# Dense experts by tiles of 512 text columns with two image tiles, and smaller edits around them, in a two-layer fusion kernel

## The reference

```python
# x: (16, 3, 96, 96), x_txt: (16, 512)
h = concat([patches(x) @ tok_W.T + tok_b, table[x_txt] + pe])     # (16, 548, 64)
h = h + attn0(layernorm(h))      # R = x + relu(q k.T) v ; layernorm(R + relu(R w1 + b1) w2 + b2)
h = h + moe0(layernorm(h))       # top 1 of 8, hidden 256, capacity ceil(1.25 T / 8)
# layer 1, attention
qkv = h1 @ W_qkv.T + b_qkv       # k, v normalised by head of 4, with gains and biases
kv  = einsum('bhnd,bhne->bhde', k, v) / HW
h   = h + gelu((q kv + h1) @ W_proj.T + b_proj) + h1             # h1 = layernorm(h)
# layer 1, experts
weights, top_idx = top_2(softmax(xt @ Wr + br))
xe = norm(xt) * ln_g[e] + ln_b[e]
y  = gelu(xe @ W1[e] + b1[e]) @ W2[e] + b2[e]                    # e = 0..7, hidden 256
out = h + sum of weights * y[top_idx]
```

## Time and profile before

| | us |
|---|---|
| median of 3 runs (lowest, highest) | 857.36 (856.84, 860.45) |
| profiled execution | 856.15 |
| its span | 854.3 |

### The profile page before, as it was taken

One profiled execution on the slowest core, in us unless ns is written; L12 is line 12 of the kernel. 1 busy time (PEld: TensorE's weight loads), 2 busy tenths in 40 slices (PEclk: granted clock), 3 DMA queues, 4 the chain that ended last, 5 costly groups with the idle time before them and its releaser, 6 DMA issues.

```text
span 854.3 us, 16008 instructions
## 1 busy us (share of the span) xinstructions
PE 727.0 (85%) x4863; PEld 542.2 (63%) x4863; DVE 586.5 (69%) x2216; ACT 490.5 (57%) x923; POOL 436.5 (51%) x457
## 2 busy tenths in 40 slices
PE   4599999999973399735599999999999999999994
PEld 3467777777752266524377776677767777777773
DVE  2658898998886255656777777877778777765421
ACT  1356656565622266403377777667866678775652
POOL 4743547783655400265647666576666754223321
PEclk9599999999975599955589999999999999999998
DMA  8900000000000122200112321122202222022220
GB/s 244 362 15 11 9 15 22 22 19 3 5 4 3 45 87 88 62 20 8 24 37 55 62 62 33 31 62 63 62 16 49 62 63 60 10 54 62 62 61 13
DMA packets 49534, 43.69 MB, mean 51 GB/s; under 512 B 19962, under 2 KB 45066, under 8 KB 49066
## 3 DMA queue, kind: packets, MB, share of 16 engines
q1 hardware_dynamic: 40666, 36.33, 16.6%
q0 software_dynamic: 7200, 4.17, 2.2%
q10 hardware_dynamic: 1584, 2.18, 0.8%
HBM read 31.65 MB, written 13.47 MB: 53 GB/s over the span
## 4 chain that ended last, share of the span: by engine, by line
PE 45%; DVE 14%; ACT 9%; issue 7%; DMA 0%; DVEq 0%; POOL 0%; POOLq 0%; ACTq 0%
PE psum L521 9%; PE psum L1012 8%; PE psum L1013 6%; ACT scratch L607 3%; PE psum L1199 3%; PE psum L496 2%; PE psum L990 2%; ACT L607 2%; ACT L553 2%; PE psum L983 2%; PE psum L447 2%; DVE stats L1354 2%; PE psum L1181 1%; DVE xt L680 1%; DVE mv L1357 1%
## 5 line engine op out<-in xcount | busy, mean ns | idle before, releaser
L607 ACT ACTIVATE scratch<-psum,fb 128x584 f32<-128x584 f32 x256 | 177.3, 744 | 97.8 <-PE psum L1013 95.7
L422 POOL TENSOR_TENSOR prob<-prob,scratch 128x292 f32<-128x292 f32 x112 | 81.2, 725 | 150.1 <-DVE scratch L852 145.4
L521 PE MATMUL psum<-scratch,w_fw 128*64 128x292 f32 (+1 forms) x1024 | 143.0, 401 | 0.1
L382 POOL DMA_INDIRECT uu<-expert_out,slot_i x80 | 82.9, 1036 | 86.6 <-issue 77.0
L1012 PE MATMUL psum<-kh,fw_hi 128*128 128x292 f32 x352 | 105.7, 323 | 10.8 <-ACT scratch L607 10.7
L943 POOL DMA_INDIRECT slots_buf<-xt,slot_i x80 | 81.8, 1022 | 57.6 <-DVE slot_i L1594 36.0
L521 PEld LDWEIGHTS psum<-scratch,w_fw 128*64 128x64 f32 x1024 | 89.4, 136 | 27.6 <-DVE scratch L852 5.2
L1013 PE MATMUL psum<-kh,fw_lo 128*128 128x292 f32 x352 | 93.0, 291 | 0.0
L929 POOL DMA_INDIRECT emb<-in_table,w_ids x64 | 63.0, 984 | 54.3 <-DVE stats L1354 33.2
L1012 PEld LDWEIGHTS psum<-kh,fw_hi 128*128 128x128 f32 x352 | 66.8, 190 | 27.3 <-ACT scratch L607 16.0
L1256 ACT ACTIVATE prob<-psum 128x292 f32<-128x292 f32 (+1 forms) x160 | 54.9, 396 | 30.5 <-PE psum L1066 30.5
(11 more groups left out here) (262 smaller groups left out, 1696.1 us busy)
## 6 DMA issues: line engine op xcount, KB each, us to landing
X<-share_buf SPq DMA_DIRECT2D x16, 584.0 KB, 5.9
X<-share_buf SPq DMA_DIRECT2D x16, 512.0 KB, 7.7
slots_buf<-zeros SPq DMA_DIRECT2D x8, 352.0 KB, 4.4
expert_out<-zeros SPq DMA_DIRECT2D x8, 352.0 KB, 4.2
X<-slots_buf SPq DMA_DIRECT2D x16, 128.0 KB, 2.0
expert_out<-X SPq DMA_DIRECT2D x16, 128.0 KB, 1.7
out<-H SPq DMA_DIRECT2D x16, 128.0 KB
X<-in_patches ACTq DMA_DIRECT2D x1, 1728.0 KB, 7.0
```

The costliest lines, as they stand in the source:

```text
L382: pool.indirect_dma_start(yg[b % 2][0:rows, s, :], None, expert_out, bass.IndirectOffsetOnAxis(slot_i[0:rows, b, (s + 1) % SLOTS:(s + 1) % ...
L422: pool.tensor_tensor(total[b % 2][:, 0:RIGHT], total[b % 2][:, 0:RIGHT], part[m % PARTS], ALU.add).then_inc(sem("summed"), 1)
L521: last = pe.matmul(bank(6 + n % 2)[h * D:(h + 1) * D, 0:z], w["fw2"][:, e * J + j, :], hid[(J * n + j) % (J * UNITS)][:, h, 0:z], start=(j ...
L607: act.activation(hid[(J * n + j) % (J * UNITS)], both(2 + 2 * j), ACT.Gelu, bias=fb1[:, e * J + j:e * J + j + 1]).then_inc(sem("gelu"), 1)
```

## The change

The dense experts run by tiles. A batch's 512 text columns are one tile, and the image tokens of batches 0 to 13 (2 x 252 columns) and of batches 14 and 15 (2 x 36 columns) are tiles 14 and 16 of 18. The columns in sum stay the same. An up product covers 512 columns into one bank, the halves go round over banks 2 to 5, and gelu reads 512 columns; down, weigh and the sums are 256 columns wide.

```diff
-                banks.take(pe, (2 + 2 * j, 3 + 2 * j), sem("gelu"), J * n + j + 1)
+                m = J * n + j
+                banks.take(pe, (2 + m % 4,), sem("gelu"), m + 1)
                 k = (e * J + j) * P
-                for h, z in enumerate(SIDES):
-                    last = two(pe, bank(2 + 2 * j + h)[:, 0:z], split["fw1"], xs5[b % XS5][:, h * ODD:h * ODD + z], slice(k, k + P))
-                last.then_inc(sem("up"), 1)
+                two(pe, bank(2 + m % 4)[:, 0:2 * width(t)], split["fw1"], tile_x(t), slice(k, k + P)).then_inc(sem("up"), 1)
```

```diff
+                for s in range(TXT):
+                    at0 = s % 2 * LEFT + s // 2 * P
+                    pe.matmul(bank(1)[:, s * 2 * E:(s + 1) * 2 * E], xs5[b % XS5][:, at0:at0 + P], wr_both[:], start=True, stop=True)
...
-                st(dve.tensor_tensor(lg[:], by_slot(1, E), bc(ratio[b % 2][:], E), ALU.mult))
+                st(dve.tensor_tensor(lg_pair[:], by_slot(1, 2 * E), bc(ratio[b % 2][:], 2 * E), ALU.mult))
+                st.sync()
+                st(dve.tensor_tensor(lg[:], lg_pair[:, :, 0:E], lg_pair[:, :, E:2 * E], ALU.add))
...
+                dve.tensor_tensor(xs5[b % XS5][other, cols], bank(1)[side, 0:LEFT], xs5[b % XS5][side, cols].bitcast(F32), ALU.subtract).then_inc(sem("xs5"), 1)
```

The gains of v move from a second product with a copy in front (p1_s) to two operations of own_heads on DVE. Fills are added, products of ones that nobody reads:

```diff
+        def fill(pe):
+
+            banks.left(pe, FILLED)
+            for _ in range(3):
+                pe.matmul(bank(FILLED).rearrange("p (k n) -> p k n", k=4), ones_b[:], bs(ones_b[:], 4), start=True, stop=True)
```

```diff
-        B_STEPS = [(e, c) for c in range(0, ET, 4) for e in range(E)]
+        B_STEPS = [(e, c, t) for c, t in ((0, 3), (3, 2), (5, 4), (9, 2)) for e in range(E)]
...
-        FIRST_UNITS = 2 * E
+        NEEDED_UNITS = (2 * E, 3 * E, NU)
...
+            def low_moe(_):
+                dve.wait_ge(sem("high_w"), 2)
+                dve.tensor_tensor(split["fw1"][1][:], fw1, split["fw1"][0][:].bitcast(F32), ALU.subtract).then_inc(sem("low_moe"), 1)
```

```diff
+            for k in range(KC):
+                if k % (KC // PATCH_LOADS) == 0:
+                    pe.wait_ge(sem(f"patches_in{k // (KC // PATCH_LOADS)}"), 16)
+                for h in range(2):
+                    last = pe.matmul(bank(h)[h * D:(h + 1) * D, 0:NB * N_IMG // 2], w["tok_w"][:, k, :], patches[:, k, h * NB * N_IMG // 2:(h + 1) * NB * N_IMG // 2],
...
+            act.activation(sd3[0][:, 0:1], eps_t[:, 0:1], ACT.Sqrt)
```

```diff
+        DVE_MOVED = {("add_input", 0): 3, ("add_input", 2): 0.5, ("finish", 17): 16, ("fold", 14): 2, ("fold", 15): -2, ("fold", 2): 0.75,
...
-        MOE, SQUEEZE_TWO, DOWN_LAG, GELU_LAG, WEIGH_LAG, SUM_LAG = 171.5, {}, 1.25, 0.5, 2.5, 0
+        MOE, DOWN_LAG, GELU_LAG, WEIGH_LAG, SUM_LAG, BACK_LAG, FINISH_LAG = 170, 1.5, 0.75, 2.5, -0.5, 12.75, 12
-        B_START, B_STEP, B_READY = -34.5, 2.7, -60
+        B_START, B_STEP, B_READY = -9, 2, -82
```

482 lines of the change are left out of this document (298 added, 184 removed), and 16 rows, old and new, of tables (ACT_MOVED, DVE_MOVED, PE_MOVED).

## The result

The changed kernel takes 847.75 us (median of four runs, 846.61 to 849.94) where the kernel before takes 857.87 beside it: a ratio of 0.9881, 95% interval 0.985 to 0.9911. That is 10 us faster. I had forecast 783 with a range from 750 to 815: right about the sign, wrong about the size by a factor of seven. The profiled execution of after took 848.33 us, 7.8 less than that of before.

A forecast was written before the change was run, and what follows sets the result against it. PE was taken to set the pace in phase 1 and the dense stage, a chain over four engines at half clock between. Terms -6 - 1 - 7 - 14 - 46 = -74 gave 782.2 us profiled, 783 median, range 750 to 815.

The forecast's parts named there:

- A, start: Start up to phase 1: patch products in two column groups and image tokens in halves, -6 us (-1 to -8).
- B, body: Body of phase 1: no operation changes, at most half of PE's missing 6 us returns, -1 us (0 to -3).
- C, end of the first part: End of phase 1 to first unit's turn: shorter waits, fills holding the clock up (4 us), -7 us (-2 to -11).
- D, first turn to first up: First unit's turn to first dense unit: gather waits less, clock gives 10 us, -14 us (-4, clock unchanged, to -20).
- E, dense stage: Dense stage: PE needs 21.1 us a batch, period 22.7 instead of 26.95, -46 us (-25 to -67).
- with the starts still there: Dense stage: a pair of units takes 4.4 us if slower starts remain, 3.84 without waits and starts.
- Rival 2: Dense stage: DVE operations stretched beside POOL become the bound, 3.3 us more a batch, 826 us; chance 0.20.
- Rival 3: Dense stage: latency of one batch's chain sets the period, above 28.4 us, kernel slower (872 at 29.5); chance 0.03.

The follow-up runs named there:

- e17: Kernel before with extra unused PE products in the dense stage, 5.1 us a batch: ratio 1.0939 to the kernel before, period 32.15 us.
- e7: Kernel before with ACT's roots4 moved early, beside the other Sqrt stages: ratio 1.002 to the kernel before, period 27.2 us.
- e1: Changed kernel with the first part's plan tables as before the change: 840.6 us, ratio 0.9793 to the kernel before.
- e2: Changed kernel without the 44 fills (PE products whose result nobody reads): 845.2 us, ratio 0.9854 to the kernel before.
- e13: Changed kernel with extra unused PE products in the dense stage, 5.1 us a batch: ratio 1.065 to the kernel before, period 29.06 us.
- e16: Kernel of e9 with the same extra PE products, 5.1 us a batch: ratio 1.0545 to the kernel before, period 29.25 us.
- e3: Changed kernel with ACT's roots4 moved beside the other Sqrt stages, two table loads fewer a batch: 831.6 us, ratio 0.9695 to the kernel before.
- e4: Changed kernel with square on ACT and sum_squares on DVE moved later: ratio 1.005 to the kernel before, period 26.1 us.
- e10: Changed kernel with kv on PE and kv_b on DVE moved earlier: ratio 1.0001 to the kernel before, period 26.0 us.
- e14: Changed kernel with extra unused gelus on ACT, 1.1 us a batch: ratio 1.0017 to the kernel before, period 26.0 us.
- e8: Changed kernel with the edits of e1, e2 and e5 together: ratio 0.9647 to the kernel before, period 23.8 us.
- e9: Changed kernel with the edits of e1, e2 and e3 together: 819.0 us, ratio 0.9539 to the kernel before.
- e18: Kernel before with extra unused gelus on ACT, 1.3 us a batch: ratio 1.0091 to the kernel before, period 27.7 us.
- e5: Kernel of e3 with PE's route products moved ahead of one unit's up products: ratio 0.9787 to the kernel before, period 23.9 us.
- e11: Kernel of e9 with kv and kv_b earlier as in e10: ratio 0.9643 to the kernel before, period 24.4 us.
- e12: Changed kernel with the first part's tables of DVE, ACT and POOL as before, PE's as changed: ratio 0.9932 to the kernel before.
- e15: Changed kernel with extra unused weighs on DVE, 1.0 us a batch: ratio 0.9942 to the kernel before, period 25.5 us.
- e6: Changed kernel with up products going round over two banks instead of four: ratio 1.0733 to the kernel before, period 29.8 us.

## Why the prediction was wrong, step by step

- **What bounds the kernel before** was right: PE in the dense stage (e17 passes on 5.1 of 5.1, e7 nothing).
- **A, start.** The first turn came at 19.46, 7.4 earlier, a little more than the sum had, but by other parts. The products in two column groups and halves took 2.19 and 2.77 us, 5.2 from start to end against 7.42, where half, 3.7, was forecast. They started 2.35 earlier (6.54 instead of 8.89), with the patches in three transfers, which the sum did not have. But at k_low of batch 0 only 2.5 were left, and at batch 15 in e1 0.3. The step that failed: I priced the first turn and not what is late next, which is the embeddings; DVE stood for them right behind its first norm:

```profile
21.76 0.43 DVE L1607 TENSOR_TENSOR H<-emb,w_pe 128x256 f32<-128x256 f32 x1 [2.04 <-DMA emb<-in_table,w_ids]
27.83 1.48 DVE L1607 TENSOR_TENSOR H<-emb,w_pe 128x256 f32<-128x256 f32 x1 [2.19 <-DMA emb<-in_table,w_ids]
```

- **B, body.** "No operation changes" did not carry the -1: I took a new order of the same operations for free. The body took 9.8 us more, 7.2 of them by the order (e1). This was no part of the range (0 and -3).
- **C, end of the first part.** -7 forecast, +2.4 measured. The fw1 part on DVE took 2.28 us, near the 2.6 of the estimate. The 4 us for the clock were 0 (without fills, e2, the turn comes 1.2 earlier). The path goes by place and POOL: POOL went on with batch 14's scatters until 289 and batch 15's until 295.2, and the turn follows 3.3 us behind the last scatter, as it did before (3.4). So time taken from ACT and PE ahead of place did not bring the turn forward.
- **D, first turn to first up.** -14 forecast, -5.4 measured. The wait of 4.53 us for the gather came down to 1.68 (DVE at 374.86), and the bound "with the clock unchanged -4" was the right one: of the 10 us for the clock nothing came (e2 needs 133.2 from turn to up without fills, after 135.1 with them).
- **E, dense stage.** -46 forecast, -12.0 measured, the largest miss, and the step that failed is PE's need of 21.1 us a batch. By e13 and e16 it is 23.2. The pairs of units were nearly right: in the tail a pair takes 3.95 us, 3.84 forecast and 5.08 before, from one up to the next:

```profile
828.38 0.50 PE L1140 MATMUL psum<-kh,fw_hi 128*128 128x512 f32 x1
...
832.33 0.51 PE L1140 MATMUL psum<-kh,fw_hi 128*128 128x512 f32 x1
```

  Four pairs are 15.8, so 23.2 - 15.8 = 7.4 us go to what stands beside them, where I had 5.7 after 6.6. Instead of falling it grew. Two things are in it. The 21.1 had no waits at all, but PE's waits for DVE, 0.7 us a batch before, are 1.2 in e13 (and 2.1 in after, where the downs wait twice a batch for weigh). And each change from one kind of product to another costs a start: 0.33 instead of 0.24 for the first up after anything else, and 0.31 from the last downs to the next kind, where two pairs of downs are 0.22 apart. The new order puts more of these between the units. How the rest divides is not shown. Rows of after:

```profile
618.00 0.50 PE L1140 MATMUL psum<-kh,fw_hi 128*128 128x512 f32 x1
618.33 0.39 PE L1141 MATMUL psum<-kh,fw_lo 128*128 128x512 f32 x1
618.56 0.39 PE L1140 MATMUL psum<-kh,fw_hi 128*128 128x512 f32 x1
...
620.46 1.08 PE L628 MATMUL psum<-scratch,w_fw 128*64 128x256 f32 x8 [0.34 <-DVE prob L978]
621.95 1.08 PE L628 MATMUL psum<-scratch,w_fw 128*64 128x256 f32 x8 [0.40 <-DVE scratch L978]
```

  The 4.4 for a pair "with the starts still there" would give 23.3, close to 23.2, but by luck: the pair is 3.95, and the missing time lies beside the pairs. What comes on top of PE's need was 1.6 in the forecast (21.1 / 0.93) and is 1.6 at full clock (24.8 - 23.2), but by luck too: I had priced two engines, PE and DVE, that wait for each other. It is ACT's in-order program that matters, of which I wrote that PE "lives on what its four banks hold" during table loads. It stands 6.6 us a batch in front of square and stack4, and 1.2 of the 1.6 come back with two loads gone (e3), with DVE at 89 of 100. The clock drops add 0.2 a batch. In all 25.0 instead of 22.7, 30 us over thirteen periods; the stretches outside them took 75 instead of 71. In these the clock dropped once more: the ups from 817 to 822 us start 0.43 apart instead of 0.235, 2.4 us in all.
- **Rival 2** (DVE stretched by POOL) did not come: the operation that took 0.60 in the median before takes 0.19 now, with both inputs in SBUF as before:

```profile
L929 DVE SCALAR_TENSOR_TENSOR lg<-oh,lg x16: 190/191/831, 414.4 to 778.3; 128x40 f32<-128x40 f32 x16
```

  One that is still stretched in most batches has both inputs in SBUF too (oh); a second operation of the same kind and size (oh_) never is:

```profile
L900 DVE TENSOR_TENSOR oh<-eq,qq x16: 199/455/765, 413.8 to 776.9; 128x40 f32<-128x40 f32 x16
L900 DVE TENSOR_TENSOR oh_<-eq,qq x16: 199/201/202, 419.7 to 781.9; 128x40 f32<-128x40 f32 x16
```

  The rule of the Trainium skill, "SBUF — State Buffer", section "Who interferes with whom", is about two instructions that overlap in time, and an order decides which do. The trace agrees as far as it goes: the same operation is stretched in one place and not in the other. The added operations did not raise the sum as I had priced it: DVE is busy for 21.3 us a batch, 0.4 over the forecast of 20.9, and not 3.3.
- **Rival 3** (a chain over several engines sets the period) had something of what holds the period above PE's need, with ACT's in-order program in it; but its condition (a period over 28.4) and its outcome (slower) did not come. I had given it 0.03, arguing from batch 0's latency. That a batch can pass in 57 us says nothing about an engine that serves three batches in one order. Whether there is a loop, and which hops form it, is still open: e4 and e10 disturbed the order and the clock, neither measured it.
- **Range and chances.** The bounds were each taken from what could be gained. None allowed a loss where an order was rewritten, and so the five terms together (-32 at the least) had no way to reach -8.

## What to carry to other kernels

An engine busy for 73 parts of 100 can hold up the others if its program is in order and it stands in front of something not ready while ready work is behind it. Busy shares don't tell this; add a known piece of work to each engine in turn and see how much of it is passed on, at the same granted clock. Measure the piece itself too: mine was 5.1 us where I meant 1.4. Placing stages that need the same ACT table side by side paid only where ACT was on the path (16 us after the change, nothing before it). Treat a rewritten order of unchanged operations as an edit with a price of its own, with a bound on both sides. Count a higher clock only where PE's products are what the next engine waits for. And compare two kernels stretch by stretch at the same clock, or its drops pass for effects of the edit.

## What the runs showed of the hardware that I had not expected

Six products of 256 columns onto one half of the columns cost 0.42 us each in a row (two counts of the trace each), where eight that alternate between the halves take 1.88 in all, 0.235 each: the neighbours overlap.

The granted clock also drops within the dense stage, with PE busy for over 90 parts of 100. In after the same sixteen downs that take 1.95 us took 3.47 once in the window 539 to 639:

```profile
583.79 3.47 PE L628 MATMUL psum<-scratch,w_fw 128*64 128x256 f32 x16
```

In the 25 us ahead of it PE's longest wait was 0.72 us (for route, at 580.98), the others were under half a microsecond. A period with such a drop is longer than one at full clock by 1.0 us in the mean in after, 0.9 in e14 and 1.6 to 1.7 in e10, e13 and e16. How often it comes differs from kernel to kernel: in none of ten periods in the kernel before, e3, e7, e8, e9, e17 and e18, in one to four in after, e1, e2, e5, e11, e12 and e15, in five or six in e4, e10, e13, e14 and e16, in seven in e6. In e13 it comes in every second period. A busier PE is not what decides: e17 has PE busy for 95 parts of 100 without a drop, e13 for 95 with five. What brings the drop about no run here tells.
